# An attention kernel in which each unit's sums of exponentials are totalled between the two halves of the next unit's latent queries

## The chip, the cores and the metric

The kernel runs on one core of one Trainium2 chip. The metric is device time in microseconds (us) of the whole program, the median of the runs shown. Everything below is FP32, or FP32 split into two parts (high and low) that TensorE takes as `fp32r`.

## The reference

One block of a transformer over 2048 tokens of width 512:

```python
xn = _layernorm(x)
c_Q, c_KV = xn @ W_DQ.T, xn @ W_DKV.T              # latent, width 128
q = concat(c_Q @ W_UQ.T, rope(c_Q @ W_QR.T))       # 16 heads, 128 + 64
k = concat(c_KV @ W_UK.T, rope(xn @ W_KR.T))
scores = clip(q @ k.T, -80, 80), causal
s = softmax(scores / sqrt(192)) @ v                # v = c_KV @ W_UV.T
out = x + (s @ W_O.T) * silu(ffn(xn))              # ffn: linear + 2 of 8 low-rank experts
```

The softmax needs, for every query and head, the sum of all its exponentials. How and when those sums are totalled over the keys is what this case is about.

## The kernel before

**Stages.** `prepare` (until about 145 us) normalises the rows and writes keys, values and the linear part to memory. `attend_and_combine` then does the attention, and from about 1185 us on the last projection and the output.

**Units.** Attention goes over 16 units, numbered n = 0 to 15. A unit is a couple of token tiles (256 queries) and one half (`par`) of the 16 heads, so 8 heads x 256 queries = 2048 columns, worked on as two halves of 1024. The keys are absorbed into the queries: a unit's latent queries (`q_h`, `q_l`) are made on TensorE from `cq` and `absorb` (`latent`, L1295 to L1297) while the unit before it is under way, into `score_ps`, and read from there by ScalarE (`latent_high`, L1518: the high part) and VectorE (`latent_low`, L1638: what is left). Each half is 12 matmuls of 256 columns.

**Pairs.** A unit walks over pairs of (queries, one tile of 128 keys). It starts with kind CORNER (the diagonal), goes on with LATE (the second diagonal tile, half as wide) and then, from n = 2 on, FULL pairs: the later the unit, the more of them. For each half of a pair TensorE makes scores (L1360, or L1330 to L1342), ScalarE the exponential (`exponential`, L1547), VectorE clips it (L1675 or L1680), ScalarE takes the high part (`high`, L1553), VectorE the low part (`low`, L1693) and TensorE weighs the values with both (L1382, or L1401 to L1405) into `out_ps`. VectorE also adds the exponentials to `total` (L1688); the first pair of a unit is copied there by ScalarE (`begin`, L1560).

**The end of a unit** lies inside the CORNER pair of the next one, in the function `head` on TensorE. It totals the unit before over its 128 partitions: `sum_up` (L1315) is four matmuls with a block of ones of 32 columns, which the trace shows as eight records of tile 128x32, into bank 0 of `out_ps`. ScalarE copies this bank to `sums` (`read_sums`, L1529) and raises the semaphore `sums_read`. Bank 0 is also where the CORNER pair's own weighing begins (`weigh(t, 0, ...)`, L1401), so TensorE waits for `sums_read` ahead of it. `head` of a unit with a next one does, in this order: `sum_up`, `latent` half 0, `latent` half 1, `weigh` half 0, and in all couples but the last `rotary` (L1306 to L1308), which VectorE's `turn` (L1648) reads.

**What sets the order.** Every engine runs its own list of instructions in the order of the code, and semaphores tie them together. `sweep` writes the same walk over units and pairs out for each engine. In the CORNER pair ScalarE's list is: `exponential(0)`, `read_out` (L1523, the finished half of `out_ps`), `high(0)`, `exponential(1)`, `begin(0)`, `high(1)`, `read_sums`, `latent_high` of both halves, `begin(1)`. The wait that matters below stands in `head` on TensorE:

```python
pe.wait_ge(values_in, 16 * (t + 1))
since(pe, sums_read, n)
weigh(t, 0, slot, CORNER, False)
```

Unit 0 has nothing to total. Unit 15 has no next unit and does a merge of weights (L1425) in place of latent queries. Units 1 to 14, fourteen in all, have both.

Of the kernel before, what the change touches and what calls it, by code (L numbers as in the profile page):

```python
# [942 lines left out]
def attend_and_combine(nc, block, keep, top, keys, values, turned, w_uv, w_o, heads_out, sums_out, inverses, x, linear, last_rows, out):  # L943

    ctx = ExitStack()
    with ctx:
# [22 lines left out]
        out_ps = ctx.enter_context(nc.psum_tensor("out_ps", [P, 4, 512], F32))  # L969
# [26 lines left out]
        exp_done = sem("exp_done")  # L996
# [291 lines left out]
        def _(pe):  # L1288
            def latent(couple, heads, half):

                tokens = bass.ds(couple * CT, CT)
                for h in range(HH):
                    head = heads * UHEADS + half * HH + h
                    w, out = slice(head * P, (head + 1) * P), score_ps[:, half, h * CT:(h + 1) * CT]
                    pe.matmul(out, keep.absorb_h[:, w], keep.cq_h[:, tokens], start=True, stop=False)  # L1295
                    pe.matmul(out, keep.absorb_h[:, w], keep.cq_l[:, tokens], start=False, stop=False)
                    mm = pe.matmul(out, keep.absorb_l[:, w], keep.cq_h[:, tokens], start=False, stop=True)  # L1297
                mm.then_inc(q_scored, 1)
# [109 lines left out]
            def head(t, unit, slot, prev):  # L1408

                n, par = unit.n, unit.par  # L1410
                if prev is not None:
                    pe.wait_ge(summed, unit.added)
                    pe.wait_ge(out_read[0], n)
                    sum_up(1 - par, out_ps[:, 0, :])
                if unit.has_next:
                    for half in range(2):
                        pe.wait_ge(exp_done, 2 * t + 1 + half)
                        latent(unit.next_couple, 1 - par, half)
                else:
                    pe.wait_ge(weights_in, 16 * WEIGHT_PARTS)  # L1420
                    for h in range(HEADS):
                        if h % 2 == 0 and h < 4:
                            pe.wait_ge(exp_done, 2 * t + 1 + h // 2)
                        since(pe, merge_split, h - 3)
                        pe.matmul(merge_ps[h % 4], uv[:, h, :], wo[h], start=True, stop=True).then_inc(merged, 1)  # L1425
# [3 lines that stand above are left out]
                if unit.has_second:  # L1429
                    since(pe, out_read[1], n)  # L1430
                    rotary(unit.couple + 1, par)
# [82 lines left out]
        @block.scalar  # L1514
        def _(act):
            def latent_high(unit, par, half):
                act.wait_ge(q_scored, 2 * unit + half + 1)
                nc.scalar.copy(q_h[par][:, half * HW:(half + 1) * HW], score_ps[:, half, :]).then_inc(q_high, 1)  # L1518

            def read_out(unit):  # L1520

                since(act, heads_stored, 16 * unit)
                nc.scalar.copy(head_rows[:, 0:HW], out_ps[:, 0:2, :]).then_inc(out_read[0], 1)  # L1523

            def read_sums(n, bank):

                act.wait_ge(summed_up, n + 1)
                since(act, sums_stored, 16 * n)
                nc.scalar.copy(sums[:, :], bank[:, 0:512]).then_inc(sums_read, 1)  # L1529

            def pair(t, unit, k, slot, kind, prev):
                n, par = unit.n, unit.par
                width = HW // 2 if kind == LATE else HW

                def exponential(half):
                    act.wait_ge(scored, 2 * t + half + 1)
                    since(act, split, 2 * t + half - 1)

                    if kind == LATE:
                        act.wait_ge(begun, 2 * n + half + 1)  # L1540
                    if kind == FULL:
                        act.wait_ge(summed, unit.added + 2 * k + half + 1)
                    if kind == CORNER and prev is not None:
                        act.wait_ge(summed, unit.added + half - 1)
                    if prev is None:
                        act.wait_ge(first_turned, 2)
                    nc.scalar.activation(prob[half][:, 0:width], score_ps[:, half, 0:width], ACT.Exp,  # L1547
                                         scale=QK_SCALE).then_inc(exp_done, 1)

                def high(half):  # L1550
                    act.wait_ge(clipped, 2 * t + half + 1)
                    since(act, weighed, 2 * t + half - 1)
                    nc.scalar.copy(prob_h[half][:, 0:width], prob[half][:, 0:width]).then_inc(high_done, 1)  # L1553

                def begin(half):


                    since(act, summed_up, n - 1)
                    act.wait_ge(clipped, 2 * t + half + 1)
                    nc.scalar.copy(total[par][:, half * HW:(half + 1) * HW], prob[half][:, :]).then_inc(begun, 1)  # L1560

                if kind != CORNER:
                    for half in range(2):
                        exponential(half)
                        high(half)
                    if closes(unit, kind, k, 3):
                        high_half(0, 0, 0)
                    if closes(unit, kind, k, 2):
                        high_half(0, 0, 1)
                    first_couple = isinstance(unit.couple, int) and unit.couple == 0  # L1570
                    if unit.has_second and (kind == LATE and first_couple or
                                            kind == FULL and isinstance(k, int) and k == 1):
                        since(act, passed_high, 16 * n)
                        act.wait_ge(r_step, 4 * n + 2)
                        nc.scalar.copy(rot_hl[:, 0, :, :], rot_f[:, :, :]).then_inc(r_step, 1)
                    return
                exponential(0)
                if prev is None:
                    exponential(1)
                if prev is not None:  # L1580
                    act.wait_ge(weighed, 2 * t - 1)
                    read_out(n - 1)
                high(0)
                if prev is not None:
                    exponential(1)
                begin(0)
                high(1)
                if prev is not None:
                    read_sums(n - 1, out_ps[:, 0, :])
                if prev is None:  # L1590
                    act.wait_ge(all_values_out, 16 * GROUPS)
                if unit.has_next:
                    latent_high(n + 1, 1 - par, 0)
                    latent_high(n + 1, 1 - par, 1)
                else:
                    for h in range(HEADS):
                        act.wait_ge(merged, h + 1)
                        nc.scalar.copy(merged_h[:, h, :], merge_ps[h % 4]).then_inc(merge_high, 1)
                begin(1)

            def high_half(t, par, half):
                heads = slice(half * UHEADS, (half + 1) * UHEADS)
                act.wait_ge(scaled, 2 * t + half + 1)
                nc.scalar.copy(rows_h[par][:, heads, :], rows[par][:, heads, :]).then_inc(rows_high, 1)  # L1604

            def high_rows(t, par, n):

                since(act, projected[par], n)
                for half in range(2):
                    high_half(t, par, half)  # L1610

            def gates(par, n):
                act.wait_ge(gate_in[par], 32 * (n + 1))
                since(act, times[par], n)
                nc.scalar.activation(gate[par], lin_in[par], ACT.Sigmoid).then_inc(sigmoid, 1)

            sweep(act, pair)
            high_rows(1, 1, 0)
            high_rows(2, 0, 1)
            act.wait_ge(weighed, 2 * PAIRS - 1)  # L1620
            read_out(UNITS - 1)
            read_sums(UNITS - 1, score_ps[:, 0, DIM:2 * DIM])
            gates(0, 0)
            gates(1, 0)
            gates(0, 1)
            high_rows(3, 1, 1)
            gates(1, 1)
            with act.Fori(2, COUPLES) as n:
                for par in range(2):
                    high_rows(2 * n + par, par, n)  # L1630
                    gates(par, n)
# [253 lines left out]
```

## Time and profile before

| | |
|---|---|
| median of 3 runs | 1371.02 us (1370.32 to 1371.18) |
| the profiled execution's own time | 1370.23 us |
| its span, first to last instruction | 1368.7 us |
| TensorE busy | 1350.0 us, 99% |
| VectorE busy | 1166.5 us, 85% |
| ScalarE busy | 766.5 us, 56% |
| GpSimd busy | 133.1 us, 10% |
| granted TensorE clock | 1.000 of full speed |

The profile is one execution. A row of the timeline has the start in us, the duration in us, the engine, the line of the code, the operation, what it writes and reads, and how many instructions were merged in the row; in brackets stands how long the engine sat idle just before, and what ended that idle time. PE is TensorE's matmul, PEld its weight load (the two overlap), DVE is VectorE, ACT ScalarE, POOL GpSimd, SP the engine that issues loads. Ends of matmuls are modelled, so for TensorE the starts are compared.

### The profile page before, as it was taken

The page shows a single profiled execution, that of the slowest core. Times are in us where ns is not written, and L with a number is a line of the kernel's source. Part 1 is how long each engine was busy: PE and PEld are TensorE (multiplying, and loading weights), DVE is VectorE, ACT ScalarE, POOL GpSimd, SP SyncE. Part 2 cuts the span into 40 slices and gives each one's busy share as a digit, 9 for nine tenths or more (in the row PEclk, how much of TensorE's full clock was granted, in tenths as well). Part 3 has the DMA queues.
Part 4 walks back from the last instruction along what each step waited for, and adds up shares of the span by engine and source line. Part 5 has one row for each costly group of instructions (what it writes and reads, how often), then busy time and mean ns, then how long its engine had stood idle before and what let it go on. Part 6 is the DMA issues. An engine that isn't in the chain of part 4 may idle for free.

```text
span 1368.7 us, 28448 instructions
## 1 busy us (share of the span) xinstructions
PE 1350.0 (99%) x10146; PEld 1130.3 (83%) x10146; DVE 1166.5 (85%) x1355; ACT 766.5 (56%) x845; POOL 133.1 (10%) x193
## 2 busy tenths in 40 slices
PE   7999899999999999999999999999999999999998
PEld 6888788888888888888888888888899688878887
DVE  7767699999999999999998998999888888967664
ACT  5233666666666666666666666666666666532221
POOL 0001121111010101010000100121100010022220
PEclk9999999999999999999999999999999999999999
DMA  8334774553432424242242422454422143255552
GB/s 315 117 99 126 234 225 156 161 153 112 150 121 97 124 91 127 96 115 88 77 145 65 117 91 67 124 177 126 132 57 66 62 135 104 79 184 171 172 162 92
DMA packets 110562, 174.93 MB, mean 128 GB/s; under 512 B 9784, under 2 KB 65336, under 8 KB 107960
## 3 DMA queue, kind: packets, MB, share of 16 engines
q1 hardware_dynamic: 93832, 108.99, 25.3%
q0 software_dynamic: 16688, 65.37, 15.8%
q8 instruction: 27, 0.44, 0.1%
q14 instruction: 15, 0.12, 0.0%
HBM read 125.83 MB, written 48.50 MB: 127 GB/s over the span
## 4 chain that ended last, share of the span: by engine, by line
PE 88%; DVE 6%; ACT 3%; issue 1%; DMA 0%; DVEq 0%; ACTq 0%; SPq 0%
PE score_ps L1360 34%; PE out_ps L1382 22%; PE score_ps L1493 4%; PE score_ps L1495 4%; PE score_ps L1494 4%; PE base_ps L500 3%; PE work_ps L473 2%; PE work_ps L451 2%; DVE prob_l L1693 2%; ACT prob_h L1553 2%; PE score_ps L1295 1%; DVE prob L1680 1%; PE out_ps L1315 1%; ACT prob L1547 1%; PE score_ps L1425 1%
## 5 line engine op out<-in xcount | busy, mean ns | idle before, releaser
L1553 ACT CAST prob_h<-prob 128x1024 fp32r<-128x1024 f32 (+1 forms) x288 | 289.5, 1005 | 227.7 <-DVE prob L1675 179.0
L1360 PE MATMUL score_ps<-q_h,key_slot 64*128 64x512 f32 x1984 | 397.8, 389 | 0.0
L1382 PE MATMUL out_ps<-prob_h,value_slot 64*128 64x512 f32 (+1 forms) x1984 | 382.8, 376 | 0.7
L1547 ACT ACTIVATE prob<-score_ps 128x1024 f32<-128x1024 f32 (+1 forms) x288 | 281.9, 979 | 143.2 <-PE score_ps L1360 104.8
L1693 DVE TENSOR_TENSOR prob_l<-prob,prob_h 128x1024 fp32r<-128x1024 f32 (+1 forms) x288 | 336.0, 1167 | 16.7 <-ACT prob_h L1553 14.1
L1688 DVE TENSOR_TENSOR total<-total,prob 128x1024 f32<-128x1024 f32 (+1 forms) x256 | 294.8, 1152 | 0.0
L1382 PEld LDWEIGHTS out_ps<-prob_h,value_slot 64*128 64x128 f32 x1984 | 195.2, 184 | 37.5 <-DVE prob_l L1693 6.6
L1360 PEld LDWEIGHTS score_ps<-q_h,key_slot 64*128 64x128 f32 x1984 | 194.9, 185 | 35.6 <-issue 5.9
L1675 DVE TENSOR_SCALAR prob<-prob 128x1024 f32<-128x1024 f32 x224 | 155.3, 693 | 65.3 <-ACT prob L1547 63.0
L1360 PE MATMUL score_ps<-q_l,key_slot 64*128 64x512 f32 x992 | 198.1, 387 | 0.0
L1360 PE MATMUL score_ps<-rot_hh,key_slot 64*128 64x512 f32 x992 | 198.1, 387 | 0.0
L1382 PE MATMUL out_ps<-prob_l,value_slot 64*128 64x512 f32 (+1 forms) x992 | 192.0, 375 | 0.0
L1360 PEld LDWEIGHTS score_ps<-rot_hh,key_slot 64*128 64x128 f32 x992 | 97.5, 184 | 16.5
L1382 PEld LDWEIGHTS out_ps<-prob_l,value_slot 64*128 64x128 f32 x992 | 97.7, 185 | 15.1
L1360 PEld LDWEIGHTS score_ps<-q_l,key_slot 64*128 64x128 f32 x992 | 97.6, 185 | 13.2
L1493 PE MATMUL score_ps<-merged_h,rows_h 128*128 128x512 f32 x256 | 100.1, 391 | 0.7 <-DVE rows_l L1708 0.7
L1495 PE MATMUL score_ps<-merged_h,rows_l 128*128 128x512 f32 x256 | 99.7, 390 | 0.0
L1494 PE MATMUL score_ps<-merged_l,rows_h 128*128 128x512 f32 x256 | 99.7, 390 | 0.0
L1360 PE MATMUL score_ps<-rot_l,key_slot 64*128 64x512 f32 x496 | 98.8, 386 | 0.0
L1604 ACT CAST rows_h<-rows 128x1024 fp32r<-128x1024 f32 x32 | 33.7, 1053 | 109.0 <-DVE rows L1702 107.9
L1680 DVE SCALAR_TENSOR_TENSOR prob<-prob,causal 128x1024 f32<-128x1024 f32 (+1 forms) x64 | 61.0, 954 | 12.4 <-ACT prob L1547 12.4
L159 POOL DMA_DIRECT2D rot_hh<-turned x32 | 20.6, 648 | 415.6 <-PE score_ps L1297 343.8
(230 smaller groups left out, 1800.1 us busy)
## 6 DMA issues: line engine op xcount, KB each, us to landing
key_slot<-keys SPq DMA_DIRECT2D x144, 256.0 KB, 2.6
value_slot<-values SPq DMA_DIRECT2D x144, 128.0 KB, 2.4
rot_hh<-turned POOLq DMA_DIRECT2D x32, 512.0 KB, 6.5
heads_rows<-head_rows POOLq DMA_DIRECT2D x15, 1024.0 KB, 9.6
turned<-rot_hl POOLq DMA_DIRECT2D x28, 512.0 KB, 3.0
rows<-heads_rows SPq DMA_DIRECT2D x28, 512.0 KB, 5.5
rot_l<-turned POOLq DMA_DIRECT2D x32, 256.0 KB, 7.5
linear<-y SPq DMA_DIRECT2D x4, 1024.0 KB, 4.2
```

Source lines behind the costliest of these rows:

```text
L500: mm = pe.matmul(base_ps[:, a, :], xs[:, c, a * P:(a + 1) * P], ws[:, c, 0:DIM], start=(n == 0), stop=False)
L1360: mm = pe.matmul(score_ps[:, half, c * 512:(c + 1) * 512], keys_of[ROWS[r], :], moving[par][ROWS[r], half * HW + c * 512:half * HW + (c + ...
L1382: mm = pe.matmul(out, values_of[ROWS[r], :], moving, start=False, stop=last and crossed and n == 2)
L1493: pe.matmul(sum_ps[par], rows_h[par][:, h, :], merged_h[:, h, :], start=(h == 0), stop=False)
L1494: pe.matmul(sum_ps[par], rows_h[par][:, h, :], merged_l[:, h, :], start=False, stop=False)
L1495: mm = pe.matmul(sum_ps[par], rows_l[par][:, h, :], merged_h[:, h, :], start=False, stop=(h == HEADS - 1))
L1547: nc.scalar.activation(prob[half][:, 0:width], score_ps[:, half, 0:width], ACT.Exp, scale=QK_SCALE).then_inc(exp_done, 1)
L1553: nc.scalar.copy(prob_h[half][:, 0:width], prob[half][:, 0:width]).then_inc(high_done, 1)
L1675: nc.vector.tensor_scalar(p, p, P_MIN, P_MAX, ALU.max, ALU.min).then_inc(clipped, 1)
L1680: nc.vector.scalar_tensor_tensor(out=heads, in0=heads, scalar=P_MIN, in1=limit, op0=ALU.max, op1=ALU.min).then_inc(clipped, 1)
L1688: nc.vector.tensor_tensor(sums, sums, by_head(half, kind), ALU.add).then_inc(summed, 1)
L1693: nc.vector.tensor_tensor(p_l, p, p_h, ALU.subtract).then_inc(split, 1)
```

## The change

On TensorE, in `head` of a unit that has a next one, half 0 of the latent queries now comes first, then `sum_up` of the unit before, then half 1. On ScalarE, `read_sums` stands between the two halves of `latent_high` instead of ahead of both. Where a unit has no next one nothing moves.

```diff
@@ head, on TensorE
                 n, par = unit.n, unit.par
+                if unit.has_next:
+                    pe.wait_ge(exp_done, 2 * t + 1)
+                    latent(unit.next_couple, 1 - par, 0)
                 if prev is not None:
                     pe.wait_ge(summed, unit.added)
                     pe.wait_ge(out_read[0], n)
                     sum_up(1 - par, out_ps[:, 0, :])
                 if unit.has_next:
-                    for half in range(2):
-                        pe.wait_ge(exp_done, 2 * t + 1 + half)
-                        latent(unit.next_couple, 1 - par, half)
+                    pe.wait_ge(exp_done, 2 * t + 2)
+                    latent(unit.next_couple, 1 - par, 1)
                 else:
@@ pair, on ScalarE
                 begin(0)
                 high(1)
-                if prev is not None:
+                if prev is not None and not unit.has_next:
                     read_sums(n - 1, out_ps[:, 0, :])
                 if prev is None:
                     act.wait_ge(all_values_out, 16 * GROUPS)
                 if unit.has_next:
                     latent_high(n + 1, 1 - par, 0)
+                if unit.has_next and prev is not None:
+                    read_sums(n - 1, out_ps[:, 0, :])
+                if unit.has_next:
                     latent_high(n + 1, 1 - par, 1)
                 else:
```

TensorE's list in the CORNER pair of unit 2, before (L1401 to L1405 weigh the last pair of unit 1, L1315 is `sum_up`, L1295 to L1297 are the latent queries of unit 3, four heads to a half, three matmuls to a head):

```order
L1401 MATMUL out_ps<-prob_h,value_slot 128x2x128
L1402 MATMUL out_ps<-prob_l,value_slot 128x2x128
L1405 MATMUL out_ps<-prob_h,value_slot 128x2x128
L1315 MATMUL out_ps<-total,ones 32x512 x4
L1295 MATMUL score_ps<-cq_h,absorb_h 128x256
L1296 MATMUL score_ps<-cq_l,absorb_h 128x256
L1297 MATMUL score_ps<-cq_h,absorb_l 128x256
```

and now, from the fourth head on:

```order
L1295 MATMUL score_ps<-cq_h,absorb_h 128x256
L1296 MATMUL score_ps<-cq_l,absorb_h 128x256
L1297 MATMUL score_ps<-cq_h,absorb_l 128x256
L1315 MATMUL out_ps<-total,ones 32x512 x4
L1295 MATMUL score_ps<-cq_h,absorb_h 128x256
L1296 MATMUL score_ps<-cq_l,absorb_h 128x256
L1297 MATMUL score_ps<-cq_h,absorb_l 128x256
```

The four matmuls of `sum_up` have moved behind twelve of the 24 latent ones; twelve still follow them, and then L1401.

ScalarE's list at the same kind of place (CORNER pair of unit 1), before:

```order
L1547 ACTIVATE prob<-score_ps 128x1024
L1560 COPY total<-prob 128x1024
L1553 CAST prob_h<-prob 128x1024
L1529 COPY sums<-out_ps 128x512
L1518 CAST q_h<-score_ps 128x1024 x2
L1560 COPY total<-prob 128x1024
```

and now (every line number of ScalarE's part is higher by 2):

```order
L1549 ACTIVATE prob<-score_ps 128x1024
L1562 COPY total<-prob 128x1024
L1555 CAST prob_h<-prob 128x1024
L1520 CAST q_h<-score_ps 128x1024
L1531 COPY sums<-out_ps 128x512
L1520 CAST q_h<-score_ps 128x1024
L1562 COPY total<-prob 128x1024
```

The copy of the sums has moved behind one of the two casts of the latent queries. VectorE's, GpSimd's and the loading engine's lists are the same as before.

## Rows read from the trace of the kernel before

**Rows 1.** The page: busy time by engine, and the chain that ended last.
```profile
PE 1350.0 (99%) x10146; PEld 1130.3 (83%) x10146; DVE 1166.5 (85%) x1355; ACT 766.5 (56%) x845; POOL 133.1 (10%) x193
PE 88%; DVE 6%; ACT 3%; issue 1%; DMA 0%; DVEq 0%; ACTq 0%; SPq 0%
```

**Rows 2.** The waits: engine, what waited, for what: us in total, times, longest.
```profile
PEld out_ps L1315 <- DVE total L1688: 4.3, 11, 0.5
```

**Rows 3.** The timeline of unit 7's CORNER pair, TensorE.
```profile
391.99 0.39 PE L1382 MATMUL out_ps<-prob_h,value_slot 64*128 64x512 f32 x2
392.31 0.16 PEld L1315 LDWEIGHTS out_ps<-total,ones 128*32 128x32 f32 x8 [0.35 <-DVE total L1688]
393.31 0.39 PE L1295 MATMUL score_ps<-cq_h,absorb_h 128*128 x1
...
394.85 0.28 PE L1295 MATMUL score_ps<-cq_h,absorb_h 128*128 x1
...
396.29 0.40 PE L1401 MATMUL out_ps<-prob_h,value_slot 128*128 128x512 f32 x1
396.52 0.40 PE L1402 MATMUL out_ps<-prob_l,value_slot 128*128 128x512 f32 x1
```

**Rows 4.** The timeline of TensorE where no total is waited for: unit 15.
```profile
1070.38 0.39 PE L1405 MATMUL out_ps<-prob_h,value_slot 128*128 128x512 f32 x1
1070.70 0.16 PEld L1315 LDWEIGHTS out_ps<-total,ones 128*32 128x32 f32 x8 [0.35 <-issue]
```

**Rows 5.** The timeline of ScalarE in unit 7's CORNER pair.
```profile
395.37 0.58 ACT L1529 COPY sums<-out_ps 128x512 f32<-128x512 f32 x1
395.85 1.93 ACT L1518 CAST q_h<-score_ps 128x1024 fp32r<-128x1024 f32 x2
397.65 1.07 ACT L1560 COPY total<-prob 128x1024 f32<-128x1024 f32 x1
```

**Rows 6.** The timeline of unit 1's CORNER pair, where TensorE already waits for the sums.
```profile
170.40 0.58 ACT L1529 COPY sums<-out_ps 128x512 f32<-128x512 f32 x1
171.07 0.47 PE L1401 MATMUL out_ps<-prob_h,value_slot 128*128 128x512 f32 x1 [1.46 <-issue]
171.38 0.39 PE L1402 MATMUL out_ps<-prob_l,value_slot 128*128 128x512 f32 x1
```

**Rows 7.** The timeline of unit 12's CORNER pair.
```profile
765.32 0.57 ACT L1529 COPY sums<-out_ps 128x512 f32<-128x512 f32 x1
766.30 0.40 PE L1401 MATMUL out_ps<-prob_h,value_slot 128*128 128x512 f32 x1
```

**Rows 8.** The timeline of VectorE and ScalarE behind it, units 7 and 12.
```profile
396.90 2.36 DVE L1638 TENSOR_TENSOR q_l<-score_ps,q_h 128x1024 fp32r<-128x1024 f32 x2 [0.17 <-ACT q_h L1518]
...
405.82 1.03 ACT L1547 ACTIVATE prob<-score_ps 128x1024 f32<-128x1024 f32 x1 [0.79 <-DVE prob_l L1693]
...
409.51 0.39 PE L1360 MATMUL score_ps<-rot_l,key_slot 64*128 64x512 f32 x2
409.98 0.50 PE L1382 MATMUL out_ps<-prob_h,value_slot 64*128 64x512 f32 x2
...
769.45 0.69 DVE L1648 TENSOR_TENSOR prod<-out_ps,cos 128x512 f32<-128x512 f32 x1 [0.25 <-PE out_ps L1308]
...
775.84 1.03 ACT L1547 ACTIVATE prob<-score_ps 128x1024 f32<-128x1024 f32 x1 [0.67 <-PE score_ps L1360]
```

**Rows 9.** The timeline of unit 14's CORNER pair and the scores behind it.
```profile
962.02 0.57 ACT L1529 COPY sums<-out_ps 128x512 f32<-128x512 f32 x1
963.15 0.40 PE L1401 MATMUL out_ps<-prob_h,value_slot 128*128 128x512 f32 x1
964.87 0.47 PE L1330 MATMUL score_ps<-q_h,key_slot 128*128 128x512 f32 x1 [0.17 <-issue]
```

**Rows 10.** The timeline of TensorE in unit 3, the longer wait for a total.
```profile
215.29 0.44 PE L1382 MATMUL out_ps<-prob_h,value_slot 64*128 64x512 f32 x2
215.86 0.16 PEld L1315 LDWEIGHTS out_ps<-total,ones 128*32 128x32 f32 x8 [0.55 <-DVE total L1688]
```

## The prediction

> **What bounds the kernel now.** I read the busy shares first: TensorE is busy for 1350.0 of 1368.7 us, and of the chain that ended last 88% is its own [rows 1]. So nothing is to be had but in the 1.4% in which TensorE stands still, and everything that makes it stand still longer is paid in full, unless it is given back at a later wait. Then I read the waits. One of TensorE's longest is `sum_up` for the last addition to `total`: 4.3 us in eleven places [rows 2]. It is the wait at which the change is aimed, so I asked of the timeline what it is worth.
>
> Less than it looks. In unit 7 the last weighing starts at 391.99 and `sum_up` at 392.31, a step of 0.32 us [rows 3]; steps between matmuls of that width are 0.23 us (396.29 to 396.52 in the same rows). In unit 15, where the idle time is put down to no one, the very same step is 0.32 us and the very same idle time 0.35 us [rows 4]. So 0.09 us of it come with the change from one tile size to another, and the wait for VectorE costs nothing beyond that. Units 5 to 14 all look like unit 7. Only units 3 and 4 have a longer step, 0.57 us in unit 3 [rows 10], so 0.25 us more each. Units 1 and 2 have no such wait. What can be gained at `sum_up` is thus about 0.5 us in the whole program.
>
> Last I read what stands behind `sum_up`. L1401 writes into the bank that holds the totals, so it waits until ScalarE has copied them (`sums_read`). In unit 1 this wait is there to be seen: TensorE is idle for 1.46 us and starts at 171.07, ScalarE's copy of the sums starts at 170.40 and takes 0.58 us [rows 6]. From the copy's start to L1401's start are 0.67 us. Units 2, 3 and 4 have the same 0.67 to 0.68 us: they are gated by the copy too. In units 5 to 14 the copy comes just early enough: L1401 starts 0.92 us behind its start in unit 7 [rows 3, 5], 0.98 us in unit 12 [rows 7]. So this copy has 0.25 to 0.31 us to spare, in the best case.
>
> **The change, part by part.**
>
> 1. *The copy of the sums on ScalarE moves behind one cast of latent queries.* ScalarE's list runs through without a gap there: the copy at 395.37, two casts from 395.85, the next at 397.65, so a cast takes (397.65 - 395.85) / 2 = 0.90 us of its time [rows 5]. What starts the series is the cast `prob_h` ahead of it, which hangs on VectorE's clip and not on the moved instructions, so the series begins where it did. The copy starts 0.90 us later and L1401 can't start before old copy start + 0.90 + 0.67 = + 1.57 us. For the cast itself half 0 is ready: it is made first now.
>  - Units 1 to 4, gated already: 0.90 us later each, 4 x 0.90 = 3.6 us.
>  - Units 5, 7, 9, 11, 13, like unit 7: 1.57 - 0.92 = 0.65 us each, 3.25 us.
>  - Units 6, 8, 10, 12, like unit 12: 1.57 - 0.98 = 0.59 us each, 2.4 us.
>  - A matmul that starts after an idle spell is followed by the next 0.31 us later and not 0.23 [rows 3, 6]. Nine units get this anew: 9 x 0.08 = 0.7 us.
>  - Unit 14 has no `rotary`, and its next scores wait for VectorE's low part of the latent queries, at 964.87 [rows 9]. L1401 moves from 963.15 to 962.02 + 1.57 = 963.59; six matmuls at 0.23 us and the slow start of 0.08 give 965.05 for the scores, 0.18 us later than now, of which the slow start that is there now (0.08) goes away: 0.1 us.
>
> 2. *`sum_up` on TensorE moves between the halves.* Before, the array goes from tile 64x128 (or 128x128) to 128x32 and on to 128x128. Now it goes to 128x128 first, then to 128x32, then back: one change more. Its price: 0.09 us in the step [rows 4], and the second matmul of a new series comes 0.10 us late (twelve latent matmuls take 394.85 - 393.31 = 1.54 us in half 0, and 396.29 - 394.85 = 1.44 us in half 1 [rows 3]). Together 0.2 us per unit. So TensorE alone would come to L1401 of unit 7 at 396.49, but it may start only at 395.37 + 1.57 = 396.94: the 0.2 us lie inside the new wait and cost nothing. If ScalarE weren't late, they would cost 14 x 0.2 = 2.8 us.
>
>  The Trainium skill says the same of such a move (TensorEngine Tiling (Array Packing), Key Properties): changing the tiling mode drains TensorE. By that rule alone the move costs time and wins none, and the time would be that of rival 1. The trace agrees: there is the step of 0.32 us with nothing to wait for.
>
> 3. *The waits.* The wait for `summed` goes away, since twelve matmuls (1.5 us) now run ahead of it: that is the 2 x 0.25 us of units 3 and 4, and both units are held by the copy anyway, so it gives nothing. The waits for `exp_done` keep their cover: half 1 of the latent queries starts 2.9 us after the last weighing now (394.85 - 391.99 [rows 3]), and 0.1 us later than that in the new order.
>
> 4. *VectorE.* It now waits 0.17 us for the first half of the latent queries [rows 8]; that half will be there early. The next thing on its list, `turn`, needs TensorE's `rotary`, which stands behind L1401 and comes later with it. So the 0.17 us are not kept: VectorE waits at `turn` instead.
>
> Is the delay given back further on? The next wait of TensorE is at 409.98, 0.47 us after a matmul where 0.23 would do, 0.24 us [rows 8]. Between the delayed L1401 and that wait stands an exponential at 405.82, 9.53 us behind L1401 in unit 7; in unit 12 it is 775.84 - 766.30 = 9.54 us, although VectorE's `turn` started 0.13 us later there, counted from L1401 [rows 3, 7, 8]. So what follows keeps its distance to L1401, and moves with it as a whole.
>
> The sum: 3.6 + 3.25 + 2.4 + 0.7 + 0.1 = 10.0 us. Against the profiled execution's own 1370.2 us this is 1380.2 us. The median of the runs shown is 0.8 us above that execution, so I say **1381.0 us**, slower by 0.7%.
>
> **The rivals.**
>
> *1. The copy isn't late, only the extra change of tile is paid.* That would be so if TensorE came to L1401 later than I think, or ScalarE's series began earlier. For it: the tile change is in the rows. Against it: the series starts from VectorE's clip, which nothing moves. Price: 2.8 - 0.5 = 2.3 us, 1373.3 us. Chance 0.06.
>
> *2. It gets faster.* One mechanism: the release of TensorE at the start of `head`. If the 0.09 us before `sum_up` in twelve units are the wait for the total after all, and the 0.34 us in units 3 and 4, then 12 x 0.09 + 2 x 0.34 = 1.8 us go, and with VectorE's 0.17 us in 14 units, 2.4 us more. It decides only if L1401 isn't held by the copy in any unit, that is if ScalarE reaches the copy over 0.6 us earlier than now. That gives 1371.0 - 4.2 = 1366.8 us. Against it: unit 15 [rows 4] shows the 0.09 us without a wait, and unit 1 [rows 6] shows the copy holding TensorE. Chance 0.04.
>
> *3. Part is given back.* If VectorE and ScalarE don't move along, the 0.24 us at the wait at 409.98 swallow part of it in ten units (4 to 13): 2.4 us less, 1378.6 us. Against it: the equal distances of units 7 and 12. Chance 0.07.
>
> *4. The tile change isn't hidden but adds up,* since ScalarE's casts wait in turn for TensorE: 2.8 us more, 1383.8 us. Against it: half 0 will be ready well over 1 us before its cast. Chance 0.06.
>
> **How the numbers follow.** My forecast has 0.77. It and rivals 3 and 4 are slower by over 0.2%, which is 2.7 us and about what a measurement of this kernel can tell from no change: 0.77 + 0.07 + 0.06 = 0.90. Rival 1 is 2.3 us, within 0.2%: 0.06. Rival 2 is 4.2 us on the other side: 0.04. The range runs from just under rival 3 to rival 4, 1378.0 to 1384.0 us. It leaves out rivals 1 and 2 (0.10), and some chance that my terms are each off by a third.
>
> **What would show it.** In the profile after, L1401 of each of units 1 to 14 should start with a wait of about 0.45 us in units 5 to 13 and of 2.2 us in unit 1 (1.46 + 0.90 - 0.2), put down to ScalarE's copy or to "issue"; the copy should start 0.90 us later, counted from the cast `prob_h`; the wait of `sum_up` for `total` should be gone from the list of waits; `sum_up` should be followed and preceded by a gap of the weight load in every unit. From L1382 ahead of `head` to L1401 unit 7 should take 4.95 us, now 4.30. I am wrong if L1401 starts less than 0.4 us later than now, counted like that, or if the delay is there but the pairs behind it are shorter by as much.

## The result, and the profile after

| | before | after |
|---|---|---|
| median of the runs | 1370.70 us (6 runs, 1370.32 to 1371.18) | 1382.31 us (6 runs, 1381.14 to 1382.99) |
| profiled execution | 1370.23 us, span 1368.7 us | 1382.99 us, span 1381.5 us |
| mean granted TensorE clock | 1.000 | 0.998 |

The ratio of after to before is 1.0083, with a 95% interval of 1.0072 to 1.0094: the change makes the kernel 11.6 us slower. The forecast was 1381.0 us in a range from 1378.0 to 1384.0.

The page of the kernel after, busy time and the chain that ended last, beside [rows 1]:

```profile
PE 1356.1 (98%) x10146; PEld 1121.9 (81%) x10146; DVE 1164.0 (84%) x1355; ACT 766.6 (55%) x845; POOL 132.8 (10%) x193
PE 90%; DVE 4%; ACT 3%; issue 2%; DMA 1%; ACTq 0%; SPq 0%; DVEq 0%
```

The counts are unchanged: nothing was added. TensorE's share falls and "issue" in the chain rises. The waits of TensorE after, where [rows 2] had `sum_up` waiting for the total:

```profile
PEld out_ps L1401 <- issue: 12.5, 16, 2.5
...
PEld out_ps L1315 <- issue: 0.4, 1, 0.4
...
PE out_ps L1401 <- issue: 9.0, 13, 2.4
```

The wait for `total` is gone, as it had to be, and L1401, the first weighing behind `sum_up`, has 9.0 us of idle time in 13 places. Before, the same list had this for it:

```profile
PE out_ps L1401 <- issue: 1.9, 2, 1.5
```

Nobody is named as its releaser. Who it is stands in the timeline of unit 7 after, to be laid beside [rows 3, 5] (on ScalarE lines are 2 higher than before: L1555 is the cast `prob_h`, L1520 the cast of latent queries, L1531 the copy of the sums):

```profile
399.30 0.39 PE L1382 MATMUL out_ps<-prob_h,value_slot 64*128 64x512 f32 x2
399.62 0.38 PE L1295 MATMUL score_ps<-cq_h,absorb_h 128*128 x1
401.24 1.07 PE L1315 MATMUL out_ps<-total,ones 128*32 128x512 f32 x8
401.73 1.05 ACT L1555 CAST prob_h<-prob 128x1024 fp32r<-128x1024 f32 x1 [0.36 <-DVE prob L1685]
402.23 0.38 PE L1295 MATMUL score_ps<-cq_h,absorb_h 128*128 x1
402.68 1.01 ACT L1520 CAST q_h<-score_ps 128x1024 fp32r<-128x1024 f32 x1
403.58 0.59 ACT L1531 COPY sums<-out_ps 128x512 f32<-128x512 f32 x1
404.27 0.47 PE L1401 MATMUL out_ps<-prob_h,value_slot 128*128 128x512 f32 x1 [0.34 <-issue]
407.35 0.69 DVE L1653 TENSOR_TENSOR prod<-out_ps,cos 128x512 f32<-128x512 f32 x1 [1.00 <-PE out_ps L1308]
410.95 0.19 PEld L1360 LDWEIGHTS score_ps<-q_h,key_slot 64*128 64x128 f32 x2 [0.36 <-issue]
413.86 1.03 ACT L1549 ACTIVATE prob<-score_ps 128x1024 f32<-128x1024 f32 x1 [0.80 <-DVE prob_l L1698]
```

The same cast in unit 7 before, which no row above shows:

```profile
394.42 1.05 ACT L1553 CAST prob_h<-prob 128x1024 fp32r<-128x1024 f32 x1 [0.35 <-DVE prob L1680]
```

Read it from the cast `prob_h`. The copy of the sums starts 1.85 us behind it (403.58 - 401.73), where it was 0.95 us (395.37 - 394.42): 0.90 us later. L1401 starts 0.69 us behind the copy. That distance is the same in all fourteen units now, 0.68 to 0.69 us. Before it was 0.67 or 0.68 in units 1 to 4 alone, and 0.91 to 1.13 in the others. From the last weighing ahead of `head` to L1401 it takes 4.97 us, was 4.30. And VectorE, which comes to `turn` early, stands still there for 1.00 us. The weight load of the next scores (L1360), where the tile changes once more, is idle for 0.36 us, as before (0.36 us at 402.91).

**Unit by unit.** The next table counts the start of L1401 in each unit from one common point, the first weighing of unit 0 (150.45 us before, 151.25 after: 0.80 us of the two spans' difference is made ahead of it, in the stage that the change doesn't touch). The last column ends at `sum_up` in unit 15. "More" is after less before, and "added here" what this unit adds to it.

| unit | before | after | more | added here |
|---|---|---|---|---|
| 1 | 20.62 | 21.54 | 0.92 | 0.92 |
| 2 | 38.86 | 40.68 | 1.82 | 0.90 |
| 3 | 69.42 | 73.67 | 4.25 | 2.43 |
| 4 | 99.97 | 105.12 | 5.15 | 0.90 |
| 5 | 144.07 | 149.89 | 5.82 | 0.67 |
| 6 | 188.21 | 194.64 | 6.43 | 0.61 |
| 7 | 245.84 | 253.02 | 7.18 | 0.75 |
| 8 to 13, each | | | | 0.67 to 0.77 |
| 13 | 714.27 | 725.73 | 11.46 | |
| 14 | 812.70 | 824.63 | 11.93 | 0.47 |
| 15, `sum_up` | 920.25 | 931.82 | 11.57 | -0.36 |

All of the 11.6 us is here: of the 12.8 us by which the two spans differ, 0.80 are made ahead of the attention, 11.57 in it and 0.4 behind it. One line stands out: unit 3 adds 2.43 us where 0.90 would be in keeping with its neighbours. The busy time by stretches (span of the stretch; then busy us and instructions of PE, PEld, DVE, ACT and POOL; then the granted clock, the DMA share and GB/s) shows why, first before, then after:

```profile
190.00:195.00 5.00, 5.00 (x31) 4.40 (x30) 4.84 (x7) 2.59 (x4) 2.27 (x4) 1.00 0.97 210
195.00:200.00 5.00, 5.00 (x45) 3.99 (x45) 4.47 (x8) 2.77 (x4) 0.00 (x0) 1.00 1.01 324
```

```profile
192.00:193.00 1.00, 1.00 (x4) 0.82 (x5) 1.00 (x2) 1.00 (x2) 0.47 (x1) 0.77 1.04 299
193.00:194.00 1.00, 1.00 (x4) 0.81 (x3) 1.00 (x1) 0.69 (x1) 0.14 (x1) 0.50 1.00 205
194.00:195.00 1.00, 1.00 (x6) 0.90 (x6) 0.01 (x1) 0.00 (x0) 0.00 (x0) 0.50 1.00 287
195.00:196.00 1.00, 1.00 (x7) 1.00 (x6) 0.00 (x0) 0.00 (x0) 0.00 (x0) 0.53 1.07 348
```

Between about 192.5 and 196 us the granted clock is 0.50, the lower of its two levels, 1.2 GHz in place of 2.4. TensorE is shown busy all that time, but a matmul of 512 columns takes 0.63 us there, where it takes 0.40 us in [rows 3]:

```profile
193.26 0.63 PE L1402 MATMUL out_ps<-prob_l,value_slot 128*128 128x512 f32 x1
```

This is right behind the stall of unit 2. A stall is a time in which TensorE stands idle. The two longest of the attention are those ahead of L1401 in units 1 and 2. Both are longer than before, where they were 1.46 us (unit 1, [rows 6]) and 0.46 us:

```profile
172.79 0.47 PE L1401 MATMUL out_ps<-prob_h,value_slot 128*128 128x512 f32 x1 [2.37 <-issue]
191.93 0.47 PE L1401 MATMUL out_ps<-prob_h,value_slot 128*128 128x512 f32 x1 [2.15 <-issue]
```

So there were two things to test: that ScalarE's copy makes the delay, and TensorE's new order doesn't, and that the low clock comes from those two stalls and costs 1.5 us (2.43 less 0.90), which the forecast had not.

### The profile page after: what moved, and what is told of

Same layout as the page of the kernel before. It is cut to its first block, busy times and chain, and to the rows that moved or that the text cites. A ratio compares the mean times of both kernels' runs of the same rounds, so it can differ in the third digit from the quotient of the medians.

```text
span 1381.5 us, 28448 instructions
## 1 busy us (share of the span) xinstructions
PE 1356.1 (98%) x10146; PEld 1121.9 (81%) x10146; DVE 1164.0 (84%) x1355; ACT 766.6 (55%) x845; POOL 132.8 (10%) x193
## 4 chain that ended last, share of the span: by engine, by line
PE 90%; DVE 4%; ACT 3%; issue 2%; DMA 1%; ACTq 0%; SPq 0%; DVEq 0%
PE score_ps L1360 34%; PE out_ps L1382 23%; PE score_ps L1495 4%; PE score_ps L1497 4%; PE score_ps L1496 4%; PE base_ps L500 3%; PE work_ps L473 2%; PE work_ps L451 2%; ACT prob_h L1555 1%; DVE prob_l L1698 1%; PE out_ps L1401 1%; PE score_ps L1295 1%; PE out_ps L1405 1%; PE out_ps L1402 1%; PE out_ps L1315 1%
## 5 line engine op out<-in xcount | busy, mean ns | idle before, releaser
L1555 ACT CAST prob_h<-prob 128x1024 fp32r<-128x1024 f32 (+1 forms) x288 | 289.6, 1005 | 227.7 <-DVE prob L1680 178.9
L1360 PE MATMUL score_ps<-q_h,key_slot 64*128 64x512 f32 x1984 | 393.1, 389 | 0.0
L1382 PE MATMUL out_ps<-prob_h,value_slot 64*128 64x512 f32 (+1 forms) x1984 | 378.0, 376 | 0.7
L1382 PEld LDWEIGHTS out_ps<-prob_h,value_slot 64*128 64x128 f32 x1984 | 190.4, 184 | 40.5 <-DVE prob_l L1698 6.7
L1360 PEld LDWEIGHTS score_ps<-q_h,key_slot 64*128 64x128 f32 x1984 | 190.2, 184 | 38.6 <-issue 6.0
L1360 PE MATMUL score_ps<-q_l,key_slot 64*128 64x512 f32 x992 | 195.8, 387 | 0.0
L1360 PE MATMUL score_ps<-rot_hh,key_slot 64*128 64x512 f32 x992 | 195.7, 387 | 0.0
L1360 PEld LDWEIGHTS score_ps<-rot_hh,key_slot 64*128 64x128 f32 x992 | 95.0, 184 | 18.0
L1360 PEld LDWEIGHTS score_ps<-q_l,key_slot 64*128 64x128 f32 x992 | 95.2, 185 | 14.7
L1360 PE MATMUL score_ps<-rot_l,key_slot 64*128 64x512 f32 x496 | 97.6, 386 | 0.0
```

What stands on the lines that cost most here:

```text
L1360: mm = pe.matmul(score_ps[:, half, c * 512:(c + 1) * 512], keys_of[ROWS[r], :], moving[par][ROWS[r], half * HW + c * 512:half * HW + (c + ...
L1382: mm = pe.matmul(out, values_of[ROWS[r], :], moving, start=False, stop=last and crossed and n == 2)
```

## The experiments

Every experiment is an edit of the kernel before. Beside the medians I give the count of the table above, from unit 0's first weighing to `sum_up` of unit 15, less that of the kernel before (920.25 us). It is one profiled execution each, but it leaves out what differs ahead of the attention, which moves a run's time by 1 us or so: the kernel before gave 1369.03 to 1372.07 us in the 27 runs of the first four experiments.

### ScalarE's half of the change alone

```diff
                 begin(0)
                 high(1)
-                if prev is not None:
+                if prev is not None and not unit.has_next:
                     read_sums(n - 1, out_ps[:, 0, :])
...
                     latent_high(n + 1, 1 - par, 0)
+                if unit.has_next and prev is not None:
+                    read_sums(n - 1, out_ps[:, 0, :])
+                if unit.has_next:
                     latent_high(n + 1, 1 - par, 1)
```

> Only ScalarE's part of the change: the copy of the sums between the two casts, TensorE's order as before. Copy theory: L1401 is held by the copy, which comes 0.90 us later, so all of the 10.0 us stay, and a low clock behind the long stalls of units 1 and 2 may come on top as in the changed kernel (1.5 us): 1380.7 to 1382.3 us. Tile theory (the loss is TensorE's extra change of tile size): nothing is added on TensorE, 1370.7 us.

Measured: 1382.80 us against 1370.78, ratio 1.0085 (1.0072 to 1.0099). The count is 931.93, 11.7 us more. This half alone does all of it, the low clock included (0.78 in the stretch from 192 us, then 0.50, 0.50 and 0.51). The median is 0.5 us above the range that was expected, whose upper end lies within the interval. The copy theory holds; the tile theory falls. In unit 7 the copy starts at 403.89, and L1401 again 0.69 us behind it:

```profile
404.58 0.47 PE L1401 MATMUL out_ps<-prob_h,value_slot 128*128 128x512 f32 x1 [0.52 <-issue]
```

TensorE is idle for 0.52 us there; in the changed kernel it is 0.34 us. The difference is what TensorE's own new order takes, and it lies inside the wait.

### TensorE's half of the change alone

```diff
+                if unit.has_next:
+                    pe.wait_ge(exp_done, 2 * t + 1)
+                    latent(unit.next_couple, 1 - par, 0)
                 if prev is not None:
...
                 if unit.has_next:
-                    for half in range(2):
-                        pe.wait_ge(exp_done, 2 * t + 1 + half)
-                        latent(unit.next_couple, 1 - par, half)
+                    pe.wait_ge(exp_done, 2 * t + 2)
+                    latent(unit.next_couple, 1 - par, 1)
```

> Only TensorE's part of the change: sum_up between the two halves of the latent queries, ScalarE's order as before. Copy theory: the copy is as early as it was, units 1 to 4 are held by it as before, and in units 5 to 14 the extra change of tile size shows for what it costs, 0.2 us each: 2.0 us, 1372.7 us. Tile theory (the loss is made on TensorE): nearly all of the 11.6 us, 1382 us. Faster-release theory (the wait for the total was worth something): under 1370.0 us.

Measured: 1372.52 us against 1370.78, ratio 1.0008 (0.9999 to 1.0017). The runs alone can't tell this from no change, so the trace has to. The count is 921.80, 1.55 us more. Its timeline in unit 7:

```profile
392.89 0.39 PE L1382 MATMUL out_ps<-prob_h,value_slot 64*128 64x512 f32 x2
393.21 0.38 PE L1295 MATMUL score_ps<-cq_h,absorb_h 128*128 x1
...
396.27 0.58 ACT L1531 COPY sums<-out_ps 128x512 f32<-128x512 f32 x1
...
397.36 0.40 PE L1401 MATMUL out_ps<-prob_h,value_slot 128*128 128x512 f32 x1
```

From the last weighing to L1401 it takes 4.47 us, was 4.30: the extra change of tile size costs 0.17 us, nowhere near the 0.67 us of the whole change. Units 5 to 14 add 0.13 to 0.23 us each. In units 1 to 4 together it adds 0.03 us, since the copy holds them. The first step is again 0.32 us, ahead of a matmul that waits for no total, which agrees with the reading that the "wait for the total" in [rows 3] was a change of tile size. The wait that the change set out to remove was worth nothing.

### The copy one step earlier

```diff
                 begin(0)
-                high(1)
                 if prev is not None:
                     read_sums(n - 1, out_ps[:, 0, :])
+                high(1)
```

> The opposite move: order of before on TensorE, but ScalarE's copy of the sums one step earlier, ahead of the cast prob_h of half 1 and not behind it. Copy theory: in units 1 to 4 TensorE is no longer held at L1401, which gives back 1.46 us in unit 1, 0.46 in unit 2 and about 0.1 in units 3 and 4, 2.1 us in all, 1368.6 us; the 0.16 to 0.20 us by which the cast is later in some units lie in cover of the latent matmuls. If the copy doesn't hold TensorE there (the rows say issue): 1370.7 us. If the later cast of half 1 is on the path: 14 x 0.15 = 2.1 us slower, 1372.8 us.

Measured: 1370.13 us against 1370.78, ratio 0.9997 (0.9988 to 1.0006): the runs can't tell it from the kernel before. The count is 919.43, 0.8 us less. The trace shows where the rest of the 2.1 us went, in unit 1:

```profile
168.55 0.59 ACT L1529 COPY sums<-out_ps 128x512 f32<-128x512 f32 x1
...
169.30 0.41 PE L1401 MATMUL out_ps<-prob_h,value_slot 128*128 128x512 f32 x1
...
172.83 0.47 PE L1330 MATMUL score_ps<-q_h,key_slot 128*128 128x512 f32 x1 [0.53 <-issue]
...
178.22 0.47 PE L1330 MATMUL score_ps<-q_h,key_slot 128*128 128x512 f32 x1 [0.94 <-ACT prob L1547]
```

L1401 comes at 19.02 us from the common point, was 20.62: TensorE is free 1.6 us earlier, a little more than expected. But at unit 2 only 0.76 us of that is left (38.10 against 38.86). TensorE now waits 0.53 us at the LATE scores and 0.94 us, was 0.69 (the start at 178.53 before), for the exponential before unit 2. So the copy did hold TensorE, as the theory says; what stands next in line is VectorE's and ScalarE's series for the LATE pair, and it gained only 0.25 us (VectorE's `turn` starts 23.50 us from the common point, was 23.75). My 2.1 us left that out.

### The clock: both units, one, the other, neither

The whole change under a condition on the unit, the same on both engines:

```diff
+                moved = unit.has_next and prev is not None and isinstance(n, int) and n in (1, 2)
```

and the same with `n == 1`, with `n == 2`, and with the first two units left out instead.

Units 1 and 2:

> The whole change, but in units 1 and 2 alone; units 3 to 15 as before. Copy theory without a clock effect: 2 x 0.90 = 1.8 us, 1372.5 us. With the clock theory (the two stalls of over 2 us close to each other let the granted clock fall to half for 3.4 us right behind unit 2, which costs 1.5 us): 3.3 us, 1374.0 us, and a granted clock under 0.9 between about 192 and 196 us.

Measured: 1373.65 us against 1370.78, ratio 1.0017 (1.0008 to 1.0026). The count is 923.69, 3.44 us more, and L1401 of unit 3 comes 3.33 us late. Its stretches behind unit 2:

```profile
192.00:193.00 1.00, 1.00 (x4) 0.81 (x3) 1.00 (x2) 1.00 (x2) 0.54 (x1) 0.50 1.02 238
193.00:194.00 1.00, 1.00 (x4) 0.72 (x4) 0.40 (x1) 0.09 (x1) 0.00 (x0) 0.50 0.99 197
194.00:195.00 1.00, 1.00 (x7) 1.00 (x6) 0.00 (x0) 0.00 (x0) 0.00 (x0) 0.60 1.12 254
```

Unit 3 has its old order here, and yet it adds 1.53 us (3.33 at its L1401, 1.80 at that of unit 2). That is the price of the low clock by itself.

This is one execution of eleven, and the mean granted clock of each run (given to three digits) says that they are not all like it. A stretch of 3.4 us at half the clock takes 1.7 us in 1373 off the mean, 0.0012, so a run shown at 1.000 had none. Three runs are: 1370.80, 1372.25 and 1372.52 us. The other eight are shown at 0.999 or 0.998; their median is 1373.77 us, 1.5 us above the 1372.25 of the three. A run at 0.999 can owe that to the program's end, where the clock falls too (up to 1.4 us of the span in the ten traces), so the eight need not all have had it. The same two stalls bring the low clock in some runs, by the times in most, and not in all.

Unit 1 alone:

> The whole change in unit 1 alone. Copy theory: 0.9 us, 1371.7 us. Clock: unit 1's stall is 2.4 us, unit 2's stays 0.5 us. If one long stall is enough, or if the one at unit 1 is what counts, the clock falls and 1.5 us come on top (1373.2 us). If it takes both stalls, or unit 2's is what counts, the clock stays at 1.00.

Measured: 1371.76 us against 1370.70, ratio 1.0008 (0.9999 to 1.0017); count 921.04, 0.79 us more. No low clock in the attention of the profiled execution. Its two stalls:

```profile
172.06 0.47 PE L1401 MATMUL out_ps<-prob_h,value_slot 128*128 128x512 f32 x1 [2.38 <-issue]
190.28 0.47 PE L1401 MATMUL out_ps<-prob_h,value_slot 128*128 128x512 f32 x1 [1.42 <-issue]
```

Unit 2 alone:

> The whole change in unit 2 alone. Copy theory: 0.9 us, 1371.7 us. Clock: unit 1's stall stays 1.5 us, unit 2's is 2.1 us at the place where the clock fell right behind it. If unit 2's stall is what counts, a granted clock of half speed for some us behind it and 1.5 us on top (1373.2 us). If it takes both in full length, the clock stays at 1.00.

Measured: 1371.18 us against 1370.70, ratio 1.0007 (0.9998 to 1.0016); count 921.05, 0.80 us more, no low clock either. Its two stalls are shown as 1.46 and 1.67 us: unit 2's is shorter than the 2.1 us that were expected, so this run doesn't test the second stall in its full length.

Units 3 to 14:

> The whole change, but only in units 3 to 14; units 1 and 2 as before. By the copy theory and the working of the prediction: 10.0 less 1.8 us, 8.2 us, 1379.0 us. The clock theory says that no low clock is left, since no stall of TensorE reaches 2 us and the longest new one is about 0.8 us: granted clock 1.00 everywhere in the attention. If the low clock came from the new stalls of all units, it is still there: 9.7 us, 1380.5 us.

Measured: 1379.03 us against 1370.70, ratio 1.0061 (1.0048 to 1.0075); count 928.70, 8.45 us more where 8.2 were expected (units 3 and 4 add 0.95 us each), no low clock in the attention, and all five runs at a mean clock of 1.000.

Together: unit 1 alone 0.79, unit 2 alone 0.80, both 3.44, an excess of 1.85 us. Counted at L1401 of unit 3, right behind the low clock, the excess is 1.5 us (3.33 less 0.88 and 0.94); the other 0.3 us are drifts of about 0.1 us in each of the three counts. Without a low clock the parts add up to the forecast: 0.79 + 0.80 + 8.45 = 10.04 us.

The profiled execution had the low clock in the three kernels in which both units had the late copy (the changed kernel, ScalarE's half, units 1 and 2), and not in those in which one of them or neither had. The other runs show less clear a line. Of the changed kernel's six and ScalarE's half's five runs none is at 1.000, of those of units 1 and 2 three are. Of the eleven runs with unit 1 alone, the slowest, 1373.80 us, is at 0.998. That takes more than 4 us at half the clock, which the program's end doesn't give. So most likely a low clock came in the attention there too, without unit 2's late copy. What is shown is that two long stalls make the low clock frequent, and not that it takes both. What exactly the chip looks at is not shown: lengths of the stalls, the distance between them and their time of coming were not varied one by one.

### The cost doubled

```diff
-                if prev is not None:
+                if prev is not None and not unit.has_next:
                     read_sums(n - 1, out_ps[:, 0, :])
...
                     latent_high(n + 1, 1 - par, 0)
                     latent_high(n + 1, 1 - par, 1)
+                if unit.has_next and prev is not None:
+                    read_sums(n - 1, out_ps[:, 0, :])
```

> The suspected cost doubled: TensorE's order as before, ScalarE's copy of the sums behind both casts of the latent queries. Copy theory: the copy is 1.80 us late instead of 0.90 us, so unit by unit 0.90 us more than with ScalarE's half of the change alone, in units 1 to 14: 14 x 0.90 = 12.6 us more, or 22.7 us over the kernel before without a clock effect, 1393.5 us; with a low clock behind unit 2, and perhaps behind more units as the stalls are longer, 1.5 us or more on top, 1395 to 1400 us. If the delay saturates (something behind gives it back): under 1388 us.

Measured: 1399.12 us against 1370.70, ratio 1.0203 (1.0189 to 1.0217), and a count of 948.66, 28.4 us more. The delay doesn't saturate. Its timeline in unit 7:

```profile
408.59 1.05 ACT L1553 CAST prob_h<-prob 128x1024 fp32r<-128x1024 f32 x1 [0.35 <-DVE prob L1684]
...
411.56 0.59 ACT L1529 COPY sums<-out_ps 128x512 f32<-128x512 f32 x1
...
412.25 0.47 PE L1401 MATMUL out_ps<-prob_h,value_slot 128*128 128x512 f32 x1 [1.64 <-issue]
```

The copy starts 2.97 us behind the cast, was 0.95: 2.02 us late and not 1.80. In units 1 to 4 it is 1.81 us late, as expected. From unit 5 on the second cast of latent queries comes 0.2 us late as well: in unit 7 it starts at 410.65, after 0.10 us of idle time, and TensorE's last matmul of half 1, which it reads, starts only at 410.34. L1401 again starts 0.69 us behind the copy. The low clock appears twice here, behind the stalls of units 1 and 2, of 3.28 and 3.05 us:

```profile
175.00:180.00 5.00, 5.00 (x25) 4.61 (x25) 2.43 (x5) 0.60 (x1) 0.00 (x0) 0.72 0.98 322
...
195.00:198.00 3.00, 3.00 (x11) 2.52 (x11) 0.64 (x1) 0.37 (x1) 0.61 (x1) 0.50 1.03 218
```

By the counts of L1401 in units 2 and 3 they cost about 1.3 and 1.5 us. Without these 2.8 us the count is 25.6 us more, where 22.7 were expected: units 5 to 13 add 1.75 to 2.0 us each, expected about 1.6, above all for the later second cast. The stalls of units 3 and later, 1.7 us and less, bring no low clock.

## Why the prediction was right, and what it left out

The forecast was 10.0 us over the kernel before, measured 11.6 us. By its own steps:

1. *What bounds the kernel.* Right: a delay of TensorE in the middle of the program was paid at the end. That the wait for the total costs nothing beyond the change of tile size was read from unit 15, and TensorE's half alone shows the same step.
2. *The copy moves behind one cast, 0.90 us, and L1401 follows by 0.67 us.* Measured 0.90 and 0.69 us.
 - Units 1 to 4, forecast 0.90 us each: 0.92, 0.90, 0.90 (unit 3, its 2.43 less the 1.53 us of the clock, which the run with units 1 and 2 alone shows), 0.90 us.
 - Units 5 to 13, forecast 0.65 or 0.59 us and 0.08 us for the slow start: 0.73 and 0.67. Counted from L1401 to L1401 they add 0.61 to 0.77 us, alternating as forecast.
 - Unit 14, forecast 0.1 us in the end: 0.47 us at L1401, of which 0.36 us is given back before unit 15, 0.11 us left.
3. *TensorE's new order is hidden.* Forecast 0.2 us per unit, hidden; measured 0.17 us where nothing hides it, and with ScalarE's half alone the kernel is as slow as with both, TensorE's wait at L1401 being longer by just that (0.52 us against 0.34 in unit 7).
4. *VectorE's 0.17 us aren't kept.* Right: it waits 1.00 us at `turn` instead. Nothing of the delay was given back at the next wait of TensorE: from L1401 to the exponential behind it are 9.59 us in unit 7 (413.86 - 404.27), were 9.53; the 0.06 us are about the slow start.
5. *What the sum lacked* is the clock. It had 10.0 us; without the low clock the counts give 11.57 - 1.53 = 10.04 us, and the parts of the change, run by themselves, the same 10.04. The step that fell short is the one that set the price of the stalls of units 1 and 2 at their own length, 0.90 us each. They cost 0.90 us each and, together, 1.5 us more, for a clock at half its rate for 3.4 us. The prediction put this at nothing without a word. That the range holds the result is in part luck: it went up to 1384.0 for rival 4, which didn't happen, and the forecast of 1381.0 stood on 1371.02 us for the kernel before, whose median over six runs is 1370.70.

Of the signs that it named, the copy 0.90 us later, the wait for the total gone and 4.95 us from the last weighing to L1401 in unit 7 (measured 4.97) came true. The idle time shown ahead of L1401 is 2.37 us in unit 1, forecast 2.2, and 0.27 to 0.35 us in units 5 to 13, forecast 0.45. The weight load's gap behind `sum_up` is 0.84 us, and the one ahead of it only 0.13.

Of the rivals, the first and the second need L1401 free of the copy; no unit is. The third, part given back, has nothing to show but unit 14's 0.36 us, which was in the sum. The fourth would have given nearly the measured time, 1383.8 us, for a wrong reason: the tile change was hidden, and unit 7, for one, adds 0.75 us and not 0.93 (0.65, 0.08 and 0.2).

## What to carry to other kernels

A wait in the profile's list is worth only what the step around it is longer than the same step where nobody waits: compare the two before moving work to remove it. When an instruction is moved behind another on one engine, look for who waits for its result, and how close behind it that one starts now: here the copy had 0.25 to 0.31 us to spare in units 5 to 13, and was moved by 0.90. A stall of TensorE of 2 us or more may cost more than its own length: here it did, by the times in most runs, where a second one followed 19 us later. And one profiled execution isn't all of them: look at the granted clock of every run before saying when it falls.

## What the runs showed that was not expected

- The granted clock fell to 0.50 for 3.4 us in the midst of the attention, less than 1 us after the end of a stall of 2.15 us (2.32 us with the change in units 1 and 2 alone) that came 19 us behind one of 2.37 us. In the profiled executions with stalls of 2.4 and 1.4 us, or of 1.5 and 1.7 us, at the same places, it stayed at 1.00. A stall of 3.3 us at the first of the two places was followed by a low clock by itself. With the same kernel it came in some runs and not in others: three of eleven with units 1 and 2 changed had none.
- Freeing TensorE from a wait of 1.46 us gave 1.6 us at that place and 0.76 us one unit later: the next wait in line was already 0.7 us long.
